# One block for three stages of a transformer layer pair: hand-overs by semaphores, and a new order of two steps in the first stage

## The reference, cut to what matters

```
x = x + L0_xattn(layernorm(x), ctx)    # scores c*q, softmax over the 64 context rows, second softmax over
                                       # each batch's row maxima, [c, c2q, c*c2q, c*q2c] @ W_l.T + b_l
x = x + L0_ffn(layernorm(x))           # gate -> best 2 of 8 experts per row (128 -> 512 -> 128, gelu),
                                       # plus a shared expert for every row
x = x + L1_xattn(layernorm(x), ctx)    # 16 heads of 64: q, k, v, softmax, output projection
x = x + L1_ffn(layernorm(x))           # relu feed-forward 128 -> 512 -> 128
```

## Time and profile before

| what | value |
|---|---|
| median of 3 runs | 1334.38 us (1331.47 to 1335.37) |
| profiled execution | 1321.62 us, span 1320.0 us |
| mean granted clock of PE | 0.982 |
| PE busy | 1254.1 us, 95% of the span |
| DVE / ACT / POOL busy | 992.0 / 796.2 / 525.0 us (75% / 60% / 40%) |
| stage 1 | 0 to 311.8 us, its barrier released at 311.8 |
| stage 2 | 311.8 to 569.8 us |
| stage 3 | 569.8 to 1320 us |

### The profile page before, as it was taken

How to read it: one execution, slowest core, us unless ns; L and a number is a source line. 1 busy time by engine, 2 the same in 40 slices (tenths; PEclk the granted TensorE clock), 3 DMA queues, 4 the chain that set the end, 5 groups by cost and what they waited for, 6 DMA issues and landing times.

```text
span 1320.0 us, 44086 instructions
## 1 busy us (share of the span) xinstructions
PE 1254.1 (95%) x17244; PEld 1111.5 (84%) x17245; DVE 992.0 (75%) x2446; ACT 796.2 (60%) x1552; POOL 525.0 (40%) x557
## 2 busy tenths in 40 slices
PE   6899999985999999989899999999999999999987
PEld 5788888875999999977788888888888888888867
DVE  4888888875655555538788788888877887788884
ACT  4566677733655555556666766666666666666653
POOL 2466666662212212157444424433453345243100
PEclk9899999987999999989999999999999999999999
DMA  3124423204222222130110111011011101110000
GB/s 108 66 82 143 139 88 96 78 37 148 80 73 79 74 77 77 58 89 24 30 34 14 34 34 35 14 31 38 14 34 30 38 11 34 35 34 18 2 10 18
DMA packets 86536, 71.21 MB, mean 54 GB/s; under 512 B 25088, under 2 KB 73216, under 8 KB 86368
## 3 DMA queue, kind: packets, MB, share of 16 engines
q1 hardware_dynamic: 74768, 42.71, 11.2%
q0 software_dynamic: 11600, 26.10, 6.5%
HBM read 40.73 MB, written 28.05 MB: 52 GB/s over the span
## 4 chain that ended last, share of the span: by engine, by line
PE 51%; DVE 2%; ACT 1%; issue 1%; POOL 1%; DMA 0%; DVEq 0%; ACTq 0%; POOLq 0%
PE c_ps_w L83 23%; PE c_ps_w L1708 9%; PE c_ps_s L1674 5%; PE c_ps_w L1697 5%; PE c_ps_w L1725 4%; PE c_ps_w L1683 4%; PE c_ps_w L1576 1%; DVE c_shifted L2134 1%; DVE c_r_max L2133 0%; DVE c_shifted L2128 0%; DMA c_back<-sorted_y,k_y_row_of 0%; ACT c_shifted L1920 0%; PE c_ps_w L1620 0%; DVE c_r_sum L2143 0%; POOL k_X L1467 0%
## 5 line engine op out<-in xcount | busy, mean ns | idle before, releaser
L1457 POOL DMA_INDIRECT c_back<-sorted_y,k_y_row_of x112 | 117.0, 1045 | 113.7 <-PE c_ps_w L1697 64.3
L1483 POOL TENSOR_TENSOR c_rstd<-c_var,c_minus_half 128x1 f32<-128x1 f32 x64 | 35.4, 553 | 313.5 <-DVE c_var L2111 313.2
L92 POOL DMA_INDIRECT sorted_x<-a_xn,f_slot_of x128 | 128.1, 1001 | 78.3 <-PE a_ps_w L909 36.2
L1708 PEld LDWEIGHTS c_ps_w<-c_wo,c_o_t 128*128 128x128 f32 x1024 | 122.6, 193 | 22.2 <-issue 10.9
L1200 PE MATMUL d_ps_y<-e_w_all,d_h_t 128*128 x1136 | 138.5, 275 | 0.0
L1708 PE MATMUL c_ps_w<-c_wo,c_o_t 128*128 128x128 f32 x1024 | 128.5, 279 | 9.1 <-ACT c_o_t L1915 8.9
L1071 POOL DMA_DIRECT2D sorted_y<-d_y_rows x71 | 51.0, 718 | 208.2 <-DVE d_y_rows L1102 204.0
L1200 PEld LDWEIGHTS d_ps_y<-e_w_all,d_h_t 128*128 128x128 f32 x1136 | 133.4, 192 | 0.0
L1887 ACT ACTIVATE c_q_t<-c_ps_w 128x512 f32<-128x512 f32 x120 | 70.4, 603 | 80.7 <-PE c_ps_w L83 79.6
L2128 DVE TENSOR_TENSOR c_shifted<-c_ps_s,c_mask 128x1024 f32<-128x1024 f32 x64 | 78.3, 1224 | 49.4 <-PE c_ps_s L1674 48.7
L1149 ACT ACTIVATE d_h_t<-d_ps_h,d_biases 128x256 f32<-128x256 f32 x284 | 112.2, 478 | 2.5 <-PE d_ps_h L83 2.0
(11 more groups left out here) (265 smaller groups left out, 3594.7 us busy)
## 6 DMA issues: line engine op xcount, KB each, us to landing
d_x_rows<-sorted_x SPq DMA_DIRECT2D x71, 128.0 KB, 2.1
sorted_y<-d_y_rows POOLq DMA_DIRECT2D x71, 128.0 KB, 2.2
k_X<-in_x SPq DMA_DIRECT2D x16, 256.0 KB, 3.0
a_q_rows<-in_ctx SPq DMA_DIRECT2D x16, 256.0 KB, 3.4
ctx_cols<-a_q_t SPq DMA_DIRECT2D x16, 256.0 KB, 2.3
k_ctx_raw<-ctx_cols SPq DMA_DIRECT2D x16, 256.0 KB, 2.8
out<-k_X SPq DMA_DIRECT2D x15, 256.0 KB, 3.4
sorted_x<-a_xn,f_slot_of POOLq DMA_INDIRECT x128
```

The source lines that it names most:

```text
L92: pool.indirect_dma_start(out=sorted_x, out_offset=bass.IndirectOffsetOnAxis(ap=slot_of[:, choice, t:t + 1], axis=0), in_=xn2[:, k, :], in ...
L1457: pool.indirect_dma_start(out=(back_1 if g == 1 else back)[:, choice, k, :], out_offset=None, in_=sorted_y, in_offset=bass.IndirectOffsetO ...
L1708: last = pe.matmul(w[:, 0:D], o_t[:, j, :], wo[:, j, :], start=(j == 0), stop=(j == J - 1))
```

## The change

All three stages share one block. Two semaphores take the barriers' place: `first_done`, which each of the five engines raises once at the end of stage 1 and for which PE, DVE, ACT and SP wait (value 5) before stage 2; and `experts_done`, which DVE raises when the last result row of stage 2 is made and for which ACT and POOL wait before stage 3. POOL still waits itself for scatters and stores to land. PE has no such wait before stage 3; the two banks of `ps_y` move to the front of the allocation, so that the banks PE writes first in stage 3 are those of `ps_h`. Semaphores are held to the end of the program.

In stage 1, up product 0 moves ahead of the transposes of the attention weights, and up product 2 ahead of `attend`. In the last turn with a second root (turn 16, where no group enters) that root stands ahead of the scatters of group c. At the start of stage 2, DVE makes the low part of the first x tile ahead of the third weight split.

```diff
@@ phase_a, the list of banks; PE's loop is changed alike
                 if b is not None:
                     yield ("z", b)
+                if c is not None:
+                    yield ("up", c, 0)
                 yield from (("at", a), ("bcol", a))
                 if c is not None:
-                    yield from (("up", c, j) for j in range(SC // 2))
+                    yield from (("up", c, j) for j in range(1, SC - 1))
                 yield from (("c2q", a, 0), ("c2q", a, 1))
                 if c is not None:
-                    yield from (("up", c, j) for j in range(SC // 2, SC))
+                    yield ("up", c, SC - 1)
...
-        block = ctx.enter_context(nc.Block())
...
+            sp.sem_inc(first_done, 1)
@@ phase_a, POOL
                     scatter(d, GT + 2, 2 * GT)
+                if a is None and b is not None:
+                    root2(b)
                 if c is not None:
                     scatter(c, 0, 1)
...
-                if b is not None:
+                if a is not None and b is not None:
                     root2(b)
...
             for i in range(KEPT):
                 pool.wait_ge(scattered[i], 16 * 2 * NT // KEPT)
+            pool.sem_inc(first_done, 1)
@@ phase_a, ACT
+            act.wait_ge(ratio_ready, 1)
+            act.sem_inc(first_done, 1)
@@ phase_a, PE
+            pe.wait_ge(full, len(USES))
+            pe.sem_inc(first_done, 1)
@@ phase_d
+        ps_y = [m.ps(f"ps_y{i}", [P, 512]) for i in range(2)]
         ps_h = [m.ps(f"ps_h{j}", [P, 512]) for j in range(HC)]
-        ps_y = [m.ps(f"ps_y{i}", [P, 512]) for i in range(2)]
...
-            for n in range(3):
-                copy_w1(0, n)
+            dve.wait_ge(first_done, 5)
+            copy_w1(0, 0)
+            copy_w1(0, 1)
             low_x(0, 0)
+            copy_w1(0, 2)
             low_x(0, 1)
...
+            dve.wait_ge(y_ready, N_SORTED)
+            dve.sem_inc(experts_done, 1)
@@ phase_c
+            pool.wait_ge(experts_done, 1)
             pool.memset(minus_half[:], -0.5).then_inc(half_set, 1)
...
+            act.wait_ge(experts_done, 1)
 
             act.activation(warm[:], ident[:, 0:1], ACT.Exp)
@@ build
-    with ExitStack() as ctx:
+    with ExitStack() as ctx, ExitStack() as sems, nc.Block() as block:
```

More of the change, by code:

```diff
@@ L46, with __init__ @@
 class Space:
-    def __init__(self, nc, ctx, tag):
-        self.nc, self.ctx, self.tag = nc, ctx, tag
+    def __init__(self, nc, ctx, tag, sems):
+        self.nc, self.ctx, self.tag, self.sems = nc, ctx, tag, sems
     def sb(self, name, shape, dtype=F32):
@@ L58, in sem @@
     def sem(self, name):
-        return self.ctx.enter_context(self.nc.semaphore(f"{self.tag}_{name}"))
+        return self.sems.enter_context(self.nc.semaphore(f"{self.tag}_{name}"))
 def rows(ap):
@@ L103, in phase_a @@
     with ExitStack() as ctx:
-        m = Space(nc, ctx, "a")
+        m = Space(nc, ctx, "a", sems)
         w_cq, w_q, w_c = m.sb("w_cq", [P, 1]), m.sb("w_q", [P, 1]), m.sb("w_c", [P, 1])
@@ L779, in _ @@
             weigh_choices()
+            dve.sem_inc(first_done, 1)
         @block.tensor
@@ L963, in _ @@
                     make_z(b)
+                if c is not None:
+                    feed_up(c, (0,))
                 transpose_weights(a)
                 if c is not None:
-                    feed_up(c, range(SC // 2))
+                    feed_up(c, range(1, SC - 1))
                 attend(a)
                 if c is not None:
-                    feed_up(c, range(SC // 2, SC))
+                    feed_up(c, (SC - 1,))
                 if b is not None:
                     transpose_xn(b)
+            pe.wait_ge(full, len(USES))
+            pe.sem_inc(first_done, 1)
 def batches_of(raw):
@@ L1001, in phase_d @@
     with ExitStack() as ctx:
-        m = Space(nc, ctx, "d")
+        m = Space(nc, ctx, "d", sems)
         x_rows = [m.sb(f"x_rows{i}", [P, K, D]) for i in range(RX)]
@@ L1150, in gelu @@
                                    bias=biases[c % RW][:, j:j + 1]).then_inc(h_ready, 1)
+            act.wait_ge(first_done, 5)
             act.activation(warm[:], ident[:, 0:1], ACT.Gelu)
@@ L1202, in down @@
                 last.then_inc(y_psum, 1)
+            pe.wait_ge(first_done, 5)
             transposes(0, 0)
@@ L1218, in _, with phase_c @@
             down(TURNS - 1, PEEL + U - 1)
-def phase_c(nc, T, X, layer1, w_first, w_second, y_row_of, sorted_y, ctx_cols, ctx_raw, ctx_t, ident, out):
+def phase_c(nc, block, sems, T, X, layer1, w_first, w_second, y_row_of, sorted_y, ctx_cols, ctx_raw, ctx_t, ident, out, experts_done):
     NT = X.shape[1]
@@ L1230, in phase_c @@
     with ExitStack() as ctx:
-        m = Space(nc, ctx, "c")
+        m = Space(nc, ctx, "c", sems)
         wq, wk, wv, f1 = layer1
@@ L2250, in build @@
         with ExitStack() as moe:
-            m2 = Space(nc, moe, "e")
+            m2 = Space(nc, moe, "e", sems)
             expert_of = m2.sb("expert_of", [P, N_SORTED], mybir.dt.int32)
@@ L2256, in build @@
             with ExitStack() as rest:
-                m3 = Space(nc, rest, "f")
+                m3 = Space(nc, rest, "f", sems)
                 LG = m3.sb("LG", [P, NT, E])
@@ L2264, in build @@
                 routed = (w_first, w_second, y_row_of, expert_of, tile_of)
-                phase_a(nc, T, X, LG, routing, routed, experts, sorted_x, ctx_cols, ident)
-            phase_d(nc, T, layer1, experts, expert_of, tile_of, sorted_x, sorted_y, ctx_cols, ctx_raw, ctx_t, ident, SLOTS, N_SORTED)
-        phase_c(nc, T, X, layer1, w_first, w_second, y_row_of, sorted_y, ctx_cols, ctx_raw, ctx_t, ident, out)
+                phase_a(nc, block, sems, T, X, LG, routing, routed, experts, sorted_x, ctx_cols, ident, first_done)
+            phase_d(nc, block, sems, T, layer1, experts, expert_of, tile_of, sorted_x, sorted_y, ctx_cols, ctx_raw, ctx_t, ident, SLOTS, N_SORTED, first_done, experts_done)
+        phase_c(nc, block, sems, T, X, layer1, w_first, w_second, y_row_of, sorted_y, ctx_cols, ctx_raw, ctx_t, ident, out, experts_done)
 def kernel(**inputs):
```

10 lines of the change are left out of this document (5 added, 5 removed).

## The result

| | before | changed |
|---|---|---|
| median of ten runs | 1333.16 us (1331.44 to 1335.37) | 1339.83 us (1335.98 to 1344.01) |
| ratio | | 1.0053, 95% interval 1.0036 to 1.0070 |
| profiled execution | 1321.62 us | 1344.01 us, span 1342.3, clock 0.976 |

Predicted were 1330.0 us and a range of 1324.5 to 1335.5. The change costs 7 us, half a per cent; the interval lies clear of 1.

What follows compares the result with a forecast made beforehand. PE was taken to bound stage 3, and a loop over PE, DVE and ACT stage 1's 16.73 us turn. +0.45 - 2.85 - 0.5 - 1.5 = -4.4 us, from 1334.38, gave 1330.0 us, range 1324.5 to 1335.5.

Steps and rivals of the forecast that it cites:

- The last root: End of stage 1: the early root gives back the up products' cost, but POOL's scatters become late, +0.45 us.
- group 15's first scatter follows group 14's last without a wait: End of stage 1, POOL: a sign that would show the early root working as predicted; no size of its own.
- 12.8 us between profile and median: Whole kernel: the profiled execution lies 12.8 us below the median of the runs shown, taken over as a difference.
- The up products: Stage 1 turns: ACT gets transposed weights 0.5 us later, 0.15 us late per turn, +2.5 us in all.
- cost nothing: Rival, stage 1: ACT has more slack, up products are free, the last root earns 2.1; 1327.4 us, chance 18%.
- an ACT copy of xn without idle time before it: Stage 1, ACT: sign, with turns of 16.9 us, that would prove the up products' delay.
- First seam: Between stages 1 and 2: a semaphore lets the other engines go on without POOL's DRAIN, -2.85 us.
- Start of stage 2: First x tile's low part no longer waits behind the third weight split, so the first product comes earlier, -0.5 us.
- Second seam: Between stages 2 and 3: PE starts at once, but gathers hang on POOL, released 1.5 us earlier; -1.5 us.
- the rival of the half clock: Start of stage 3: PE's clock falls during its wait for x, losing 1.2 us; 1331.2 us, chance 15%.
- slower: Rival, stage 1: ACT bounds every turn without slack, 1.0 us a turn, +12; 1339.5 us, chance 8%.
- PE's waits are the bound: Rival, stage 1: each of twelve turns gains PE's waits, 7.3 us more off; 1320.1 us, chance 7%.

Runs made afterwards that it cites:

- e4_root: The kernel before with only the last root of stage 1 moved ahead of group 14's scatters: 1340.35 us, ratio 1.0064.
- x1_let_pass: The changed kernel with POOL also waiting, before group 15's first scatter, until PE has made the last up products: 1331.89 us, ratio 0.9995.
- e7_old_root: The changed kernel with the last root back behind two scatters, everything else still changed: 1329.91 us, ratio 0.9987.
- second profile of before: The kernel before, unchanged, timed and profiled once more: 1332.96 us, ratio 0.9999; span 1330.9 us.
- b1_scores_pass: The changed kernel with the old root; in stage 1 POOL waits for the scores instead of the second product's first half: 1326.91 us, ratio 0.9964.
- b0_before_pass: The kernel before with one edit: POOL waits for the scores, not the second product's first half, before its second scatter: 1328.48 us, ratio 0.9973.
- y2_both_pauses: The changed kernel with old root, stage 1 wait for scores, and a POOL wait for first scores within stage 3's gathers: 1326.81 us, ratio 0.9962.
- e2_new_up: The kernel before with only the new places of the stage 1 up products: 1332.86 us, ratio 1.0000.
- e3_block_only: The changed kernel with old up product places, old root and old low part order, so only the single block: 1332.96 us, ratio 0.9993.
- d1_no_pass: The kernel before without POOL's four let_pass waits in a steady turn of stage 1: 1377.83 us (one run).
- x3_pe_waits: The changed kernel with the old root, and PE waiting for experts_done before stage 3's k and v products: 1331.20 us, ratio 0.9987.

## Why the prediction was wrong

**The last root: the step that failed.** The prediction put down +0.45 us for POOL being late, with -2.1 to +8 as the bounds for all of stage 1, and nothing for what POOL's unbroken row does to others. The root did start 0.1 us after its variances, and the last scatter ended 2.1 us earlier, not later. But the same edit closes the gap in POOL's scatters, and PE's increments of the last up products wait for the end of the row: +8.0 us between the last scatter and stage 2, 8 us in the time of the edit alone (`e4_root`), taken back by a pause (`x1_let_pass`) or by the old place (`e7_old_root`). I asked who waits for POOL's scatters, and not what goes on beside them. One sign that the prediction named for its success, that group 15's first scatter follows group 14's last without a wait, came true, and it is the cause of the loss.

**The profile that the sum rests on.** The prediction carried the 12.8 us between profile and median over as a constant. They are no constant: the second profile of before has a span 10.9 us longer than the first, 7.3 of it up to the last scatter, 2.0 at the start of stage 3 and 1.5 behind it. 4.6 of the 7.3 (12 turns of 0.38) go with the scores being held, which the first profile does not have and every other one has, unless POOL waits for the scores (`b1_scores_pass`, `b0_before_pass`, `y2_both_pauses`); for the rest of the 10.9 that is not shown. "Wrong if stage 1's end moves by more than 2 us" could not be read against that profile at all.

**The up products.** +2.5 us predicted, 0 measured (1.0000). ACT gets the weights late, as said: its wait for them grows from 4.3 to 10.5 us in twelve turns (`e2_new_up` against the second profile of before). The turn does not grow by it. At 17.1 us a turn one could say that the hold of DVE gives ACT slack; but in `b1_scores_pass` the turn is 16.73 us with the new places, in `b0_before_pass` 16.74 with the old. The rival "cost nothing" was right, ACT had more slack than 0.34. (The prediction worked out 0.16 to 0.26 us of lateness and took 0.15.) Its sign, an ACT copy of xn without idle time before it, could not show anything: the second profile of before has that too, with the old places. The same rival's other half, that the root then earns 2.1, was right for POOL's last scatter and wrong for the time.

**First seam.** Predicted -2.85, measured -2.0 to -2.1 (5.1 to 3.1 and 3.0 in `e3_block_only` and `e7_old_root`). Right in kind; the hand-over by semaphores costs 0.8 more than I allowed. **Start of stage 2:** -0.5 predicted, -0.4 measured, and 0 without the edit to low_x. **Second seam:** -1.5 predicted, -1.4 measured, the transposes gain 1.0 more, and PE passes without a gap (577.92 to 578.12). Here the rival of the half clock was right on place: it lies under the q products now. The changed kernel's stretch there:

```profile
591.90:598.70 6.80, 6.04 (x23) 5.47 (x24) 2.88 (x8) 3.06 (x7) 4.00 (x5) 0.50 0.31 80
```

With the hold it takes back 1.0 us in `e7_old_root` and 5.6 in the changed kernel, up to the ninth mask addition. The prediction gave this rival 1.2.

The three seam terms stand in kind: -3.9 us together where -4.85 were predicted. With the root left alone the kernel has 1329.91 us, next to the forecast of 1330.0, but that is luck. Against the runs of before beside it (median 1332.08) it is 2.2 us faster (0 to 3.3 by the interval), not 4.4: in its trace stage 3 gives back 1.0 at its start and 2.0 between the last two stores, and the forecast's 1334.38 us for before lies 2.3 above that median. The rival "slower" named 1339.5 us, and 1339.83 were measured, but it had them from ACT in every turn, which no trace shows: luck again. (The rival "PE's waits are the bound" is mis-added: 12 x (0.28 + 0.3) is 7.0, not 7.3.)

## What to carry to other kernels

A wait that seems to do nothing between POOL's indirect transfers may be what lets others' semaphores through; before an edit closes a gap in such a row, look at who hands over work during it. A wait put down to "remote", or to an engine whose work is long done, is to be laid beside POOL's timeline. And where a profile is faster than all timed runs, take another before a sum is built on it.

## What the runs showed that I had not expected

- While POOL issues indirect transfers one after the other, every 1.27 us, increments of PE's semaphores can be seen late: 0.6 us beside one scatter, 3.4 us in a row of four (`d1_no_pass`), 6 us in the row of six gathers (`x3_pe_waits`), 11 us in a row of 16. They arrive together, 0.8 to 2.2 us after the row ends. Not every increment under a scatter is held. In the second profile of before those of the last up products pass on time up to 2.4 us into the row of group 15, while that of the last product of stage 1 is recorded 4.4 us late (ended 311.18, recorded 315.57), where it costs nothing, since POOL's own end is later. In the first profile the same product's comes 0.02 us after its end (303.77, 303.79), in the same row. What decides it stays open.
- SP and PE suffer as well. SP's eight fills follow one another in 1.1 us in the first profile of before and in 3.6 to 4.3 us in the changed kernel while POOL's row lasts. PE's first scores of stage 3 take 1.16 us in the traces where they end before the row of gathers or just into it, and 2.9 to 3.6 us, the last ones three to six passes at a time with 0.4 us between, in the three where the row of six runs beside them.
- The executions that hold increments are also those whose traces lack records of them (`full`: 291 records in the first profile of before, 267 in the changed kernel). The Trainium skill (NOTIFIC — the notification-queue block, section 7.1) says that the path of the records can hold up whoever produces them. By that the hold could belong to the recording. No run here separates the two, nor says whether a kernel that records nothing has the hold; what is shown is that it is in the timed runs of this kernel (`b0_before_pass`).
- The end of a matrix product in the trace is modelled, and up to 11 us lay here between it and the moment others saw it. The Trainium skill (Perfetto Trace Analysis, section "Summary: the profiler window per engine type") lists the propagation of semaphores among what a profile does not show; the trace agrees.
- At the end of the program the clock was at half for 3.4 us in some profiles and for up to 13 us in others, with 11.3 to 13.3 us between the last two stores. Of the ten traces with one block eight have 12.9 to 13.3 us there and two 11.5; of the six with three blocks four have 11.3, the others 12.3 and 13.0. So up to 2 us may be a price of the single block that no run here tests.
